# Output product from high and low parts in an attention and mixture-of-experts layer on one Trainium2 core

## The reference

```
x = x + attention(layernorm(x))     # 16 heads of 64, keys and values from a latent of rank 128,
                                    # causal softmax, y = att @ v, then y @ w_out  (1024 x 128)
x = x + experts(layernorm(x))       # 8 experts, the best 2 of each token, silu(g) * u, down
```

## Time and profile before

| | us |
|---|---|
| median of 3 runs (lowest, highest) | 941.54 (941.38, 941.75) |
| the profiled execution, its own time | 937.43 |
| its span | 935.6 |
| PE busy (share of span) | 877.9 (94%) |
| DVE busy | 634.8 (68%) |
| ACT busy | 618.6 (66%) |
| POOL busy | 583.2 (62%) |
| mean granted TensorE clock | 0.978 of full |

### The profile page before, as it was taken

One profiled execution on the slowest core, in us unless ns is written; L12 is line 12 of the kernel. 1 busy time (PEld: TensorE's weight loads), 2 busy tenths in 40 slices (PEclk: granted clock), 3 DMA queues, 4 the chain that ended last, 5 costly groups with the idle time before them and its releaser, 6 DMA issues.

```text
span 935.6 us, 20447 instructions
## 1 busy us (share of the span) xinstructions
PE 877.9 (94%) x6126; PEld 647.6 (69%) x6127; DVE 634.8 (68%) x2386; ACT 618.6 (66%) x1614; POOL 583.2 (62%) x592
## 2 busy tenths in 40 slices
PE   6799999999999999999999999999834999999996
PEld 3566767767766776776677677676523888888885
DVE  4676687877778787777888787777852554444443
ACT  3687788678778778867877786787622555555552
POOL 3476567579467657946875794666542566555555
PEclk9999999999999999999999999999965999999999
DMA  6584430000000000000000000000011233333332
GB/s 182 190 355 185 188 101 1 1 25 13 1 16 21 1 5 21 12 2 18 19 1 4 22 12 1 19 18 2 3 35 35 41 48 48 45 45 45 45 45 26
DMA packets 43996, 44.36 MB, mean 47 GB/s; under 512 B 4352, under 2 KB 35968, under 8 KB 43920
## 3 DMA queue, kind: packets, MB, share of 16 engines
q0 software_dynamic: 16528, 26.03, 11.6%
q1 hardware_dynamic: 27392, 17.39, 6.7%
HBM read 15.28 MB, written 28.12 MB: 46 GB/s over the span
## 4 chain that ended last, share of the span: by engine, by line
PE 88%; ACT 3%; POOL 3%; DVE 3%; issue 1%; DMA 1%; POOLq 0%; SPq 0%; DVEq 0%
PE low_ps L1011 14%; PE mid_ps L939 8%; PE low_ps L998 8%; PE low_ps L1163 7%; PE mid_ps L941 6%; PE mid_ps L940 6%; PE top_ps L998 6%; PE out_ps L1018 6%; PE mid_ps L984 5%; PE top_ps L984 4%; PE out_ps L1155 4%; PE low_ps L984 4%; ACT prob L483 2%; PE top_ps L939 2%; PE top_ps L941 2%; PE top_ps L940 2%
## 5 line engine op out<-in xcount | busy, mean ns | idle before, releaser
L349 POOL TENSOR_TENSOR prob<-prob,row_inv 128x512 f32<-128x512 f32 (+3 forms) x256 | 319.5, 1267 | 219.5 <-DVE row_inv L664 219.5
L483 ACT ACTIVATE prob<-prob,neg_max 128x256 f32<-128x256 f32 (+3 forms) x512 | 280.6, 549 | 12.1 <-DVE neg_max L657 4.2
L1011 PE MATMUL low_ps<-PT,v_sb 128*64 128x512 f32 (+3 forms) x1024 | 152.0, 439 | 2.1 <-ACT PT L489 1.2
L1011 PEld LDWEIGHTS low_ps<-PT,v_sb 128*64 128x64 f32 x1024 | 68.1, 136 | 93.8 <-issue 64.4
L432 POOL DMA_INDIRECT out<-prob,meta_row x71 | 110.7, 1559 | 35.5 <-issue 34.9
L669 DVE COPY PT<-low_ps 128x512 f32<-128x512 f32 (+1 forms) x128 | 105.0, 820 | 33.8 <-PE low_ps L998 31.7
L998 PEld LDWEIGHTS low_ps<-ident,prob 128*128 128x128 f32 x640 | 74.8, 140 | 55.9 <-POOL prob L349 28.9
L896 DVE TENSOR_TENSOR prob<-mid_ps,prob 128x512 f32<-128x512 f32 x71 | 49.1, 692 | 86.7 <-ACT prob L588 53.2
L494 ACT ACTIVATE v_sb<-mid_ps 128x512 f32<-128x512 f32 x64 | 38.2, 597 | 100.1 <-PE mid_ps L941 100.0
L657 DVE CUSTOM_DVE_ANT_0 prob<-mid_ps,mask 128x128 f32<-128x128 f32 (+1 forms) x256 | 93.4, 421 | 10.5 <-PE mid_ps L984 4.5
L998 PE MATMUL low_ps<-ident,prob 128*128 128x128 f32 x640 | 91.8, 274 | 4.7 <-DVE PT L669 3.9
(11 more groups left out here) (174 smaller groups left out, 1810.4 us busy)
## 6 DMA issues: line engine op xcount, KB each, us to landing
routed_rows<-W_dn POOLq DMA_DIRECT2D x8, 2080.0 KB
routed<-routed_rows SPq DMA_DIRECT2D x71, 65.0 KB
X<-in_L_attn_x SPq DMA_DIRECT2D x8, 256.0 KB, 5.4
W_ffn<-in_L_ffn_Wg SPq DMA_DIRECT2D x8, 256.0 KB, 5.3
W_ffn<-in_L_ffn_Wu SPq DMA_DIRECT2D x8, 256.0 KB, 5.7
W_dn<-in_L_ffn_Wd SPq DMA_DIRECT2D x8, 256.0 KB, 4.5
out<-X SPq DMA_DIRECT2D x8, 256.0 KB, 2.3
out<-prob,meta_row POOLq DMA_INDIRECT x71
```

The source lines that it names most:

```text
L349: nc.gpsimd.tensor_tensor(p_pair(i), p_pair(i), row_inv[:, i, :].unsqueeze(2).to_broadcast([P, 2, P * (i + 1)]), ALU.mult).then_inc(S["nor ...
L483: nc.scalar.activation(p_at(i, h), p_at(i, h), ACT.Exp, bias=neg_max[:, i, h:h + 1], scale=-1.0, accum_out=row_sum[:, i, h:h + 1]).then_in ...
L1011: last = nc.tensor.matmul(y_ps[h * HD:(h + 1) * HD, j * P:T], v_sb[:, half, j, o + h * HD:o + (h + 1) * HD], PT[:, h, j, j:NT, :].rearrang ...
```

## The change

`y_sb` and `Wo_sb` become two float32r parts each. ACT's `y_copy` writes the high part of y. A new `y_lo` on DVE subtracts it from PSUM to make the low part. ACT makes the high part of the weights ahead of step 1 and DVE the low part inside step 1, from a raw copy that SP now loads into a free part of `v_sb`. `project_out` is three single-pass matmuls instead of one float32 matmul, and waits for `y_lo`. In ACT's step `y_copy` moves from behind the exponentials of tile 3 to ahead of them. `y_lo` stands in DVE's step ahead of `inv(n, 3)` and `t_copy(n, 1)`. After the last step `y_lo` stands ahead of the three `split_lo`. The second expert buffer moves to a part of `PT`.

```
-        Wo_sb = sb("Wo_sb", [P, NP, C])
+        Wo_sb = sb("Wo_sb", [P, 2, NP, C], F32R)
-        y_sb = sb("y_sb", [P, T])
+        y_sb = sb("y_sb", [P, 2, T], F32R)
-        hT_sb = [outT, y_sb]
+        hT_sb = [outT, PT[:, 0, 0, :, :].rearrange("p i q -> p (i q)")]
+        wo_sb = v_sb[:, 1, 2:4, :].rearrange("p a n -> p (a n)")
-            sp.dma_start(Wo_sb[:, :, :], w_out.rearrange("(g d) c -> d g c", d=P)).then_inc(wo_in, 16)
+            sp.dma_start(wo_sb.rearrange("p (g c) -> p g c", c=C), w_out.rearrange("(g d) c -> d g c", d=P)).then_inc(wo_in, 16)
             def y_copy(n):
                 seen(act, S["y_ready"], n + 1)
-                nc.scalar.activation(y_sb[:, :], y_ps, ACT.Copy).then_inc(S["y_copied"], 1)
+                nc.scalar.activation(y_sb[:, 0, :], y_ps, ACT.Copy).then_inc(S["yhi_done"], 1)
...
                 if cur:
                     exps(n, 2)
+                y_copy(n - 1)
+                if cur:
                     exps(n, 3)
-                y_copy(n - 1)
...
             w_hi(Wq, 1)
+            act.wait_ge(wo_in, 16)
+            nc.scalar.activation(Wo_sb[:, 0, :, :].rearrange("p g c -> p (g c)"), wo_sb, ACT.Copy).then_inc(S["wohi_done"], 1)
...
+            def y_lo(n):
+                seen(dve, S["yhi_done"], n + 1)
+                nc.vector.tensor_tensor(y_sb[:, 1, :], y_ps, y_sb[:, 0, :].bitcast(F32), ALU.subtract).then_inc(S["ylo_done"], 1)
...
                     post_weights(post)
+                if n == 1:
+                    dve.wait_ge(S["wohi_done"], 1)
+                    nc.vector.tensor_tensor(Wo_sb[:, 1, :, :].rearrange("p g c -> p (g c)"), wo_sb,
+                                            Wo_sb[:, 0, :, :].rearrange("p g c -> p (g c)").bitcast(F32), ALU.subtract).then_inc(S["wolo_done"], 1)
+                y_lo(n - 1)
                 if cur:
                     inv(n, 3)
                     t_copy(n, 1)
...
+            y_lo(STEPS - 1)
             split_lo(SPLIT_HI[STEPS - 1])
...
             def project_out(n, pair):
-                seen(pe, S["y_copied"], n + 1)
-                nc.tensor.matmul(out_ps[:, :], Wo_sb[:, pair, :], y_sb[:, :], start=(pair == 0), stop=(pair == NP - 1),
-                                 skip_group_check=True).then_inc(S["out_ready"], 1)
+                seen(pe, S["ylo_done"], n + 1)
+                if n == 0:
+                    pe.wait_ge(S["wolo_done"], 1)
+                for k, (a, b) in enumerate(((0, 0), (0, 1), (1, 0))):
+                    last = nc.tensor.matmul(out_ps[:, :], Wo_sb[:, a, pair, :], y_sb[:, b, :], start=(pair == 0 and k == 0),
+                                            stop=(pair == NP - 1 and k == 2), skip_group_check=True)
+                last.then_inc(S["out_ready"], 1)
...
-            pe.wait_ge(wo_in, 16)
```

More of the change, by code:

```diff
@@ L214, in layer @@
             "t0_ready", "t1_ready", "t2_ready", "t3_ready", "t0_copied", "t1_copied", "t2_copied", "t3_copied",
-            "y_ready", "y_copied", "out_ready",
+            "y_ready", "yhi_done", "ylo_done", "wohi_done", "wolo_done", "out_ready",
             "outT_copied", "outT_ready", "x2_done", "stats2", "rstd2", "xn2_done", "xn2T_ready", "xn2T_copied", "rows_copied",
```

## The result

| | before | after |
|---|---|---|
| median of 5 runs each (lowest, highest), us | 941.38 (939.96, 941.75) | 947.79 (945.69, 948.58) |
| ratio, 95% interval | | 1.0065 [1.005, 1.008] |
| profiled execution, its span, us | 937.43, 935.6 | 947.89, 946.1 |

The kernel became slower by 0.65%, about 6.4 us. A later set of five rounds with the changed kernel gave 1.009 [1.0069, 1.0111] (experiment e5).

What follows compares the result with a forecast made beforehand. PE holds 88% of the chain, but many steps run through DVE's copy freeing low_ps. Terms +1.9 - 2.2 + 4.2 - 0.7 + 1.8 + 0.1 = +5.1 on 941.54 give 946.6 us, range 942.5 to 951.5.

Steps and rivals of the forecast that it cites:

- the likeliest case: The forecast itself: the kernel slower by 5.1 us, at 946.6; chance 0.55.
- Kind A: 27 steps with little or nothing between transposes(n, 1) and the product; DVE's late copy costs 0.07 each, +1.9 together.
- V: The modelled end of a step's value product, from which the prediction measured the times within a step.
- A shorter product is worth nothing in kind A: In those steps the path runs through DVE's copy of tile 1, so the product's saving of 0.16 counts 0.
- Kind B: 14 steps (k = 3, m = 0 to 6; k = 4, m = 1 to 7) bound by the product: 0.16 saved each, -2.2.
- k = 7 loses 0.60 seven times: Steps k = 7, m = 1 to 7: y_lo pushes inv(n, 3), the copy and PE's transposes by 0.60, +4.2 together.
- k = 1 and 6, -0.05: 14 steps with a little extra PE work, between the two kinds: -0.05 each, -0.7 together.
- y_lo fits in elsewhere: Outside k = 7, y_lo was to fit DVE's time before inv, also with k = 5, without making PE's product wait.
- Step 1, +1.8: In step 1 the weights' low part on DVE, held by POOL's products, delays PE's transposes by 1.8.
- After the last step, +0.1: The last y_lo precedes the three expert low parts; 3.18 of idle time ahead of post_xn2 takes nearly all: +0.1.
- PE's time in the product, 45 us: A sign for the profile after: PE's time in the output product falls to about 45 us over 64 products.

Runs made afterwards that it cites:

- e5: The changed kernel again, unaltered, beside the kernel before: 943.64 us, ratio 1.009.
- e4: The kernel before with only ACT's y copy moved ahead of the exponentials of tile 3, float32 product kept: 941.17 us, ratio 1.0045.
- e11: The changed kernel with the high part of y copied by DVE ahead of y_lo, not by ACT: 954.88 us, ratio 1.0217.
- e2: The changed kernel with one pass instead of three in the output product, low parts still made and waited for: 945.8 us, ratio 1.0096.
- e3: The changed kernel with y_lo for k = 7 moved into post_weights, ahead of the instruction held by POOL's products: 943.91 us, ratio 1.0069.
- e6: The changed kernel with the output weights split into high and low parts in the preamble: 939.82 us, ratio 1.0059.
- e1: The changed kernel with ACT's y copy put back behind the exponentials of tile 3: 965.1 us, ratio 1.0303.
- e9: Over e6: transposes(n, 1) right behind the value product; DVE does y_copy, t_copy(n, 1), y_lo ahead of inv(n, 3), neighbouring sequences' work later: 941.58 us, ratio 1.0076.
- e12: Over e9: DVE order y_copy, y_lo, t_copy(n, 1), inv(n, 3); aggregates in front, post_weights later, scatters spread 2, 3, 3: 937.33 us, ratio 0.9975.
- e8: The kernel before, float32 product kept, with transposes(n, 1) right behind the value product and t_copy(n, 1) ahead of inv(n, 3): 932.38 us, ratio 0.9978.

## Why the prediction was right

The forecast was +5.1 and the medians differ by 6.4; the ratio of e5, 1.009, would be 8.5. Slower by more than 0.2%, as the likeliest case said, and inside its range. The mechanism held part by part. That the sum over the steps of e5, +4.78, comes so close to the forecast +5.0 is partly luck: k = 1 gained 1.5 more than reckoned, k = 7 lost 1.0 more.

- *Kind A loses 0.07.* Right: 0.06 to 0.09 in 26 of the 27 steps in e5 (in the other the kernel before was late itself), in the first profile in all but k = 8. The copy starts at V + 2.15 to 2.17 against the reckoned 2.10 to 2.12. e4 gives it for the order alone, e11 takes it away by relieving ACT.
- *A shorter product is worth nothing in kind A.* Right, and shown by e2: two passes fewer, the same place.
- *Kind B gains 0.16.* Right, 0.14 to 0.19 in twelve of the 14 steps and 0.04 in two, though only half of it lies between product and transposes (0.78 apart, before 0.86): the product itself also starts 0.08 earlier.
- *k = 7 loses 0.60 seven times.* Right, 0.65 for m = 1 to 6, with one link other than reckoned: the transposes follow the product, which waits 0.80 for y_lo, and not the copy. With one pass (e2) they do follow the copy, 0.60 late. e3 takes the delay away by y_lo's place alone. For m = 7 (step 63) it was 0.64 in the first profile and 1.29 in e5, where the clock was at its lower level.
- *k = 1 and 6, -0.05.* k = 6 -0.04. k = 1 -0.26 in e5 and -0.07 in the first profile; two such steps of before were 0.6 late themselves, so its size can't be told.
- *y_lo fits in elsewhere.* Right: outside k = 7, step 1 and the last product, PE waited for it once for 0.14 in each profile, and once for 0.70 in the first.
- *Step 1, +1.8.* Right, 1.75 and 1.73, by the held low part, which e6 moves away. The Trainium skill, "SBUF — State Buffer", section "SBUF: two separate sides", has an exclusive lock for a DVE instruction with two SBUF inputs and a GpSimd one. The rows agree: 1.89 beside POOL's products against 1.22 alone, while y_lo, with one input in PSUM, ran at its usual 0.69 beside POOL's products in e3. POOL's pair kept its 2.04 with y_lo beside it, so nothing here shows that the lock reaches y_lo.
- *After the last step, +0.1.* The cover was smaller than reckoned but held: 1.68 of 3.18 is left.
- *PE's time in the product, 45 us.* Wrong as a reading: the group shows 60.9, since each record's modelled end outlasts the start of the next. The distance of starts is what tells.
- *Not foreseen: the granted clock.* The sum left it out, and the profiles differ in it. V of step 1 stands at 41.10 (first) and 41.20 (e5), in before at 39.48, with the stretch at 0.50 that e6 shows. From V of step 63 to V of step 64 it is 10.79 (first), 14.32 (e5) and 10.20 (before); e5 got 2.3 of that back behind the last step (252.3 to the end). The timed runs differ likewise: of the 23 runs of the kernel before beside e5, the 13 with a mean clock of 0.981 or more took 931.7 to 934.1, the ten with 0.980 or less 935.5 to 938.2, and all six of e5 had 0.976 or less. By the medians of the two groups, 933.6 and 936.1, some 2.5 us of e5's distance go with the clock (an estimate; beside e1 to e4 the runs don't split like that). Whether the change brings the lower clock, by its longer stalls, or only met it, isn't shown: e4, without them, had it too.
- *Not foreseen: the k = 8 wait* of the first profile, +2.4 over the forecast, absent in e5.

Between them they can cover the 1.3 to 3.4 by which the medians exceed the forecast; which of the two did it in the timed runs, no profile shows.

## What to carry to other kernels

A step's path runs through what frees a buffer, and making the work beside it shorter shows up as idle time in front of the next instruction: look at the distance of starts, then at that instruction's releaser. A part that is computed by subtraction (high and low) adds one operation to the latency of the producer; in this kernel three passes paid only where the consumer came later than that operation, with other work on PE ahead of the product. When one wait is taken away by a new order, cost every queue that the moved work passes: e9 lost 1.2 with k = 3 by POOL's rows running into the next norms and 0.6 with k = 7 by y_lo at the end of DVE's queue, and e12 lost what it gained beside a third scatter moved into k = 1. And look at the granted clock before reading a long stretch as a wait: what made e8's last step long was a matmul at the lower clock.

## What the runs showed of the hardware

*The granted clock after a stall.* Windows of e5 behind step 63's stall, of e3 behind step 1's, of e5 behind step 1's (the third number from the right is the granted clock):

```profile
682.00:690.00 8.00, 6.80 (x28) 4.42 (x28) 1.29 (x2) 2.91 (x3) 6.31 (x8) 0.51 0.12 42
```

```profile
43.30:46.50 3.20, 3.20 (x11) 2.71 (x12) 2.03 (x4) 0.00 (x0) 2.59 (x2) 0.50 1.06 376
```

```profile
45.00:50.00 5.00, 4.64 (x40) 4.05 (x42) 3.90 (x10) 1.70 (x3) 2.59 (x2) 1.00 1.02 365
```

In e5 PE had stood idle for 3.49 ahead of the product of step 63; the clock then was 0.51, the lower of its two levels (1.2 GHz), and the three passes took 1.65 instead of 0.96. The first profile of the changed kernel has the same stall of 3.49 and kept 1.00; from V to V that step took 10.79 there and 14.32 in e5. Step 1 has the same stall of 2.14 in e3 and in e5; the clock fell to 0.50 in the one and stayed at 1.00 in the other, and from V to V the step took 13.55 and 11.97. So the same stall may or may not cost twice, here by 1.6 and 3.5 us more, of which 2.3 of the 3.5 came back behind the last step. In 11 of the 14 profiled executions, not in those of before, after and e12, the clock read 0.50 in a stretch between V of step 63 and V of step 64.

*A scatter on POOL and a maximum on DVE.* In all six steps with k = 8 of the first profile the first maximum of tile 0 waited, 1.10 in the step shown, and began within 0.04 of the end of a scatter. In the same steps of e5 it began 1.17 to 1.18 behind the start of the scores and didn't wait. The scatter began 1.19 behind that start in both steps shown, and 1.20 in the same step of the kernel before (432.48 - 431.28), where the maximum waited 0.33 and began at 432.71, in the middle of the scatter. In e12 it waited 1.80, to 0.9 past a scatter's end. Other DVE instructions, the maxima of tile 1 among them, ran during scatters without a delay, and with k = 1 in e5 tile 0 did too. So one execution has the wait in every such step and another of the same kernel in none, with the scatter in the same place to 0.02. What is shared, and what decides, isn't known from these runs.
